# Three hand-written lists of steps set anew in the sparse and dense stage of a four-block network

## The chip, the cores and the metric

The kernel runs on one core of a Trainium2 chip. The metric is the device time of one execution in microseconds, and it is the median of a few executions that counts. The engines of the core run side by side and are tied together by semaphores alone: TensorE (PE, with its weight loads as PEld), VectorE (DVE), ScalarE (ACT), GpSimd (POOL), and SyncE (SP), which issues most of the transfers.

## The reference

The input is `x` of 8 x 512 tokens by 256 channels. Four residual blocks follow one another:

```python
x = x + attn(layernorm(x))                 # 16 heads, softmax; queries outside the 60% sparsest give 0
x = x + ffn(layernorm(x))                  # router picks 4 of 16 blocks of 64 hidden units; relu
x = x + gla(layernorm(x))                  # rms norm, gated linear attention over t = 8 steps,
                                           # then a gated FFN: silu(n @ w_gate.T) * (n @ w_up.T) @ w_down.T
x = x + ffn(layernorm(x))                  # the same sparse FFN once more

def step(S, qkva):                         # the recurrence of gla, t = 0..7, for 512 rows at once
    S = a_t[..., None] * S + k_t[..., :, None] * v_t[..., None, :]
    return S, einsum('bhk,bhkv->bhv', q_t, S)
```

The recurrence runs over the first axis of `x`, which has only 8 entries, so it is computed as sums over pairs of steps.

## The kernel before

The attention stage comes first and ends at about 546 us. It is not touched. Everything behind it is `block_part`. There the work is cut into named **steps**, such as `f1.d3`. A step has one part for each engine that has something to do in it. Every engine walks the same list of names and executes its own parts in the order of that list, one after the other (`run`, L1416 to L1438). An engine never changes places in its own order: if its next part waits for a semaphore, all that stands behind it on this engine waits too. So the lists are a schedule written out by hand, and only the relative places of steps that share an engine matter.

There are three lists. `START` (L1126 to L1157, 366 steps) opens the stage, `MERGED` (L1170 to L1176, 78 steps) is the body of a loop of five rounds, and `CLOSE` (L1177 to L1186, 109 steps) ends it.

**Steps of the attention's output, groups 0 to 7 of 512 tokens, in two sets of buffers s = 0, 1.** `p{s}.mask` (DVE, `masked`, L1579 and L1581) scales and masks the attention sums into `tok[s]`. `p{s}.T` transposes it on PE (L1919), and ACT and DVE split it into a high and a low half (L1821/1823, L1627). `p{s}.wo` is 24 matmuls (L1944). `p{s}.x` adds a bias on POOL (L1484) and the result on DVE (L1590).

**Steps of the sparse FFN.** `f{s}.ln` is a layer norm on DVE (L1595 to L1603), with a power on POOL (L1445) in the middle and the add of a bias on POOL (L1490) behind it. `f{s}.T` transposes. `f{s}.rt` is the router on PE (L1973), `f{s}.lg` the choice of four on DVE (L1645 to L1657), `f{s}.mk` the transposed mask. `f{s}.m0c`, `m1c` and `m0` to `m7` are the eight hidden blocks: six matmuls and one that adds the mask (L1933, L1991), relu on ACT (L1840), low half on DVE (L1773). `f{s}.d0` to `d7` are 12 matmuls each (L1961), and `d{m}` waits for the low half of `m{m}`. `f{s}.end` adds the sum to `x` on DVE (L1636).

**Steps of the gated linear attention.** `z.ln`, `z.rms`, `z.T` normalise and transpose a block. `z.o0` to `z.o8` are nine projections in one ring of two banks: `z.o3` is the gate (`gate_in`, L1690 and L1691, on DVE), `z.o7` and `z.o8` end in a sigmoid on ACT (L1851). `og` is an output gate (24 matmuls, L1944). `rec0` to `rec7` are the recurrence. In `rec{t}` DVE first makes the product for `t + 1` (L1700), which needs the decayed keys from POOL (L1509), PE sums over heads (L2030), and DVE multiplies and reduces (L1718, L1720). `o.mean`, `o.ln`, `o.T`, `o.wo`, `o.rms` (L1613 to L1616) are what follows. `o.x` adds `x` and `y` on POOL (L1525).

**Steps of the gated FFN.** `g.m{m}` and `g.u{m}` are six matmuls each; silu on ACT (L1862), product and rounded copy on DVE (L1780, L1786), low half on POOL (L1536). `g.d{m}` waits for this low half. The steps `e.*` are those of the last block, with `e.x` for `o.x` (L1530), `e.rms` for `o.rms` and `e.gT` for `g.T`.

**Weights.** `wt0` to `wt12` round the weights of the later blocks on ACT (L1830) and take the low half on POOL (L1471). `wt2` has 18 POOL instructions more in front of it, which centre the weight `wv`. `pads` clears four small tiles on POOL (L1478 to L1480), and SP waits for it before it loads the last eight pieces, which `wt10` to `wt12` read.

In a round of the loop the gated FFN and the last sparse FFN of one block (`g.*`, `f1.*`) run beside the linear attention of the next (`z.*`, `rec*`). `rec7` and the `o.*` steps of a block stand in the round after its `rec0` to `rec6`.

Of the kernel before, what the change touches and what calls it, by code (L numbers as in the profile page):

```python
# [1108 lines left out]
def merged(a, b, places):  # L1109

    out, n = [], 0
    for k, name in enumerate(a):
        while n < len(b) and places[n] <= k:
# [12 lines left out]
START = ["p0.mask", "p1.mask", "p0.T", "p1.T", "init0", "p0.wo", "p1.wo", "p0.x", "f0.ln", "f0.T", "f0.rt",  # L1126
# [40 lines left out]

BEFORE = list(counted(START))

# [33 lines left out]

FINAL = [closing(name) for name in CLOSE]

# [995 lines left out]
```

## Time and profile before

| | |
|---|---|
| median of three executions | 1591.77 us (1589.9 to 1596.35) |
| the profiled execution | 1595.34 us |
| its span | 1593.6 us |
| PE busy | 1484.4 us, 93% |
| DVE busy | 1103.1 us, 69% |
| ACT busy | 665.2 us, 42% |
| POOL busy | 550.3 us, 35% |
| mean granted TensorE clock | 0.971 of full speed |

The profiled execution lies 3.57 us above the median, within the spread of the three. Its span begins and ends with the first and last recorded work, and 1.74 us of its time lie outside. A line of the timeline reads: start in us, duration in us, engine, line, operation, written tile <- read tiles, how often; in brackets the idle time in front of it and what ended it. Where several instructions are merged, the duration covers all of them.

### The profile page before, as it was taken

The page shows a single profiled execution, that of the slowest core. Times are in us where ns is not written, and L with a number is a line of the kernel's source. Part 1 is how long each engine was busy: PE and PEld are TensorE (multiplying, and loading weights), DVE is VectorE, ACT ScalarE, POOL GpSimd, SP SyncE. Part 2 cuts the span into 40 slices and gives each one's busy share as a digit, 9 for nine tenths or more (in the row PEclk, how much of TensorE's full clock was granted, in tenths as well). Part 3 has the DMA queues.
Part 4 walks back from the last instruction along what each step waited for, and adds up shares of the span by engine and source line. Part 5 has one row for each costly group of instructions (what it writes and reads, how often), then busy time and mean ns, then how long its engine had stood idle before and what let it go on. Part 6 is the DMA issues. An engine that isn't in the chain of part 4 may idle for free.

```text
span 1593.6 us, 25605 instructions
## 1 busy us (share of the span) xinstructions
PE 1484.4 (93%) x8904; PEld 1060.6 (67%) x8904; DVE 1103.1 (69%) x2111; ACT 665.2 (42%) x970; POOL 550.3 (35%) x696
## 2 busy tenths in 40 slices
PE   8889999999997789999988899999999999999898
PEld 7434344434332368888867587878778787878787
DVE  6777887887878755555666777767676767767542
ACT  1567767767664522223234232424334243432211
POOL 6345544546531023214320433323222332322420
PEclk9899999999997889999999999999999999999999
DMA  4323223223221211100110100001010010100001
GB/s 130 88 58 76 60 57 74 63 59 70 47 57 35 91 45 40 54 27 28 35 41 14 27 1 23 19 1 39 0 39 0 13 26 0 39 0 14 14 1 27
DMA packets 56414, 61.04 MB, mean 38 GB/s; under 512 B 15733, under 2 KB 41637, under 8 KB 56349
## 3 DMA queue, kind: packets, MB, share of 16 engines
q1 hardware_dynamic: 42653, 43.89, 10.4%
q0 software_dynamic: 13408, 16.29, 4.8%
q8 instruction: 40, 0.66, 0.2%
q14 instruction: 25, 0.20, 0.0%
q10 hardware_dynamic: 288, 0.00, 0.0%
HBM read 25.51 MB, written 8.90 MB: 22 GB/s over the span
## 4 chain that ended last, share of the span: by engine, by line
PE 48%; issue 22%; DVE 13%; POOL 9%; ACT 5%; DMA 2%; SPq 1%; POOLq 0%; DVEq 0%; ACTq 0%
PE ps L1933 11%; PE ps L1961 8%; PE ps L922 6%; PE ps L935 6%; PE ps L908 3%; POOL h L1536 3%; PE ps L865 3%; DVE mc L613 3%; POOL kT L1509 2%; PE ps L1944 2%; PE ps L877 2%; PE ps L1973 2%; PE ps L1919 1%; ACT pT0b L797 1%; DVE oT_b L1720 1%
## 5 line engine op out<-in xcount | busy, mean ns | idle before, releaser
L613 DVE TENSOR_REDUCE mc<-ps 128x2 f32<-128x1024 f32 x256 | 302.8, 1219 | 52.1 <-PE ps L908 51.9
L1961 PE MATMUL ps<-w_hi,h 128*128 128x256 f32 x1024 | 218.2, 297 | 12.2 <-DVE h L1773 12.2
L1840 ACT ACTIVATE h<-ps 128x512 fp32r<-128x512 f32 x128 | 75.5, 598 | 320.5 <-PE ps L1991 320.4
L349 POOL DMA_DIRECT2D k_st<-k_hi x256 | 124.0, 490 | 188.5 <-PE ps L922 110.3
L1961 PEld LDWEIGHTS ps<-w_hi,h 128*128 128x128 f32 x1024 | 165.5, 188 | 18.8 <-DVE h L1773 17.9
L1773 DVE SCALAR_TENSOR_TENSOR h<-ps,h 128x512 fp32r<-128x512 f32 x128 | 87.1, 689 | 127.8 <-ACT h L1840 125.0
L1933 PE MATMUL ps<-xT_b,w_hi 128*128 128x512 f32 x512 | 171.1, 415 | 0.0
L1536 POOL TENSOR_TENSOR h<-hf,h 128x512 fp32r<-128x512 f32 x56 | 72.4, 1293 | 249.7 <-DVE h L1786 249.7
L922 PE MATMUL ps<-q_st,k_st 64*128 64x512 f32 x512 | 126.1, 490 | 23.3 <-ACT pT0b L797 7.8
L1961 PE MATMUL ps<-w_lo,h 128*128 128x256 f32 x512 | 142.9, 279 | 0.0
L922 PEld LDWEIGHTS ps<-q_st,k_st 64*128 64x128 f32 x512 | 49.3, 190 | 138.0 <-ACT pT1b L797 36.8
L1509 POOL TENSOR_TENSOR kT<-kT,aT 128x128 f32<-128x128 f32 (+6 forms) x56 | 72.0, 1285 | 172.1 <-DVE pr L1700 98.6
L908 PE MATMUL ps<-k_st,q_st 48*128 48x512 f32 x512 | 109.4, 447 | 22.8 <-DVE mc L613 9.8
L1933 PEld LDWEIGHTS ps<-xT_b,w_hi 128*128 128x128 f32 x512 | 91.2, 191 | 17.9 <-issue 2.7
L1933 PE MATMUL ps<-xT_b,w_lo 128*128 128x512 f32 x256 | 102.3, 400 | 0.0
L1961 PE MATMUL ps<-w_down_b_hi,h 128*128 128x256 f32 x512 | 102.1, 284 | 0.0
L1961 PEld LDWEIGHTS ps<-w_lo,h 128*128 128x128 f32 x512 | 96.2, 188 | 2.5
L908 PEld LDWEIGHTS ps<-k_st,q_st 48*128 48x128 f32 x512 | 48.6, 188 | 72.2 <-DVE mc L613 36.6
L1933 PE MATMUL ps<-xT_b,w_gate_b_hi 128*128 128x512 f32 x256 | 83.3, 407 | 3.7 <-DVE xT_b L1627 3.1
L1961 PEld LDWEIGHTS ps<-w_down_b_hi,h 128*128 128x128 f32 x512 | 82.5, 188 | 4.5 <-POOL h L1536 2.8
L797 ACT ACTIVATE pT0a<-ps 128x1024 f32<-128x1024 f32 x64 | 65.5, 1023 | 41.2 <-PE ps L922 39.5
L797 ACT ACTIVATE pT1b<-ps 128x1024 f32<-128x1024 f32 x64 | 65.5, 1023 | 39.5 <-PE ps L922 39.4
(270 smaller groups left out, 3422.2 us busy)
## 6 DMA issues: line engine op xcount, KB each, us to landing
q_st<-q_hi SPq DMA_DIRECT2D x256, 32.0 KB, 2.1
k_st<-k_hi POOLq DMA_DIRECT2D x256, 32.0 KB, 1.9
q_st<-q_lo SPq DMA_DIRECT2D x128, 32.0 KB, 2.0
k_st<-k_lo POOLq DMA_DIRECT2D x128, 32.0 KB, 1.9
x<-in_x_dram SPq DMA_DIRECT2D x8, 512.0 KB, 4.0
x_dram<-x SPq DMA_DIRECT2D x8, 512.0 KB, 2.9
yn<-x_dram SPq DMA_DIRECT2D x16, 256.0 KB, 3.9
x<-x_dram SPq DMA_DIRECT2D x16, 256.0 KB, 3.7
```

The lines of the kernel that those rows point to most:

```text
L349: eng.dma_start((q_st, k_st)[which][par][64 * e + DH * r:64 * e + DH * r + DH, j, :].bitcast(F32), src[(2 * j + e) * DH:(2 * j + e + 1) * ...
L613: v.tensor_reduce(mc[par][:, qt, 2 * HU + j:MC:NPAIR], ps[:, at:at + 2, :], AX_X, ALU.max).then_inc(max_done, 1)
L797: a.activation(pT[p % 2][half][:, :, :], ps[:, at:at + 2, :], ACT.Exp).then_inc(exp_done, 1)
L908: last = t_.matmul(bank[2 * odd + e][:, :], q_st[par][64 * e:64 * e + 3 * DH, j, qt * P:(qt + 1) * P], k_st[par][64 * e:64 * e + 3 * DH, j ...
L922: last = t_.matmul(bank[pair_at(u, half) + e][:, :], k_st[par][64 * e:64 * e + 64, j, kt * P:(kt + 1) * P], q_st[par][64 * e:64 * e + 64, ...
L935: last = t_.matmul(o_bank[at:at + OR, :], vz[g][:, kt, HG * gr + q, :], pT[p % 2][q // 2][:, q % 2, :], start=kt == 0, stop=kt == NT - 1, ...
L1509: g.tensor_tensor(keys, keys, decay, ALU.mult).then_inc(R["kd"], 1)
L1536: g.tensor_tensor(lo[:, :], hf[s][m % 2][:, :], hi[:, :].bitcast(F32), ALU.subtract).then_inc(S["hl"], 1)
L1773: v.scalar_tensor_tensor(lo[:, :], ps[:, RING[s] + m % 2, :], 0.0, hi[:, :].bitcast(F32), ALU.max, ALU.subtract).then_inc(F[s]["hl"], 1)
L1840: a.activation(h[s][m % 2][0][:, :], ps[:, RING[s] + m % 2, :], ACT.Relu).then_inc(F[s]["relu"], 1)
L1933: last = t_.matmul(ps[:, bank, :], ws[a][:, c, m * P:(m + 1) * P], xT[s][k][:, c, :], start=n == 0, stop=close and n == NC * len(PASSES) - 1)
L1961: last = t_.matmul(ps[:, ACC[s] + t // 2, (t % 2) * D:(t % 2 + 1) * D], h[s][m % 2][a][:, t * P:(t + 1) * P], ws[k][:, m, :], start=m == 0 ...
```

## The change

No step is added, removed or altered. The three lists are replaced by permutations of themselves. `MERGED` and `CLOSE` are given whole, from `START` the stretches that the text speaks of.

```diff
 START = [
...
-         "f0.m6", "f0.d5", "f1.m0c", "wt1", "f1.mk", "f0.m7", "f0.d6", "f1.m1c", "f1.m0", "f0.d7", "f0.end",
-         "p0.mask", "f1.m1", "f1.d0", "wt2", "f1.m2", "f1.d1", "f1.m3", "p0.T", "f1.d2", "f1.m4", "p0.wo",
...
-         "f1.d7", "f0.lg", "f0.m0c", "f1.end", "f0.mk", "f0.m1c", "p1.mask", "f0.m0", "p1.T", "wt3", "f0.m1",
...
+         "f0.m6", "f1.m0c", "f1.mk", "f0.d5", "f0.m7", "f1.m1c", "f0.d6", "f1.m0", "f0.d7", "f0.end", "f1.m1",
+         "f1.d0", "f1.m2", "f1.d1", "p0.mask", "f1.m3", "p0.T", "f1.d2", "f1.m4", "p0.wo", "p0.x", "f0.ln",
+         "f1.d3", "f1.m5", "f1.d4", "f1.m6", "f0.T", "f1.d5", "f1.m7", "wt1", "f0.rt", "f0.lg", "f0.m0c",
+         "f1.d6", "f1.d7", "f1.end", "f0.mk", "f0.m1c", "p1.mask", "f0.m0", "f0.m1", "p1.T", "f0.d0", "wt2",
...
-         "p1.mask", "f0.m1c", "z.ready", "wt8", "f0.m0", "p1.T", "f0.m1", "pads", "f0.d0", "p1.wo", "f0.m2",
-         "p1.x", "f0.d1", "f0.m3", "f0.d2", "f1.ln", "f0.m4", "f0.d3", "wt9", "f0.m5", "f1.T", "z.ln", "z.rms",
-         "f0.d4", "wt10", "f0.m6", "f0.d5", "wt11", "f1.rt", "f0.m7", "f1.lg", "f1.m0c", "f0.d6", "f0.d7",
-         "wt12", "z.T", "f0.end", "f1.m1c", "f1.mk", "z.o0", "z.o1", "z.o2", "og", "z.o3", "z.o4", "f1.m0",
-         "z.o5", "z.o6", "z.o7", "z.o8", "rec0", "f1.m1", "f1.d0", "rec1", "rec2", "rec3", "f1.m2", "rec4",
-         "f1.d1", "rec5", "f1.m3", "f1.d2", "z.y", "rec6", "rec7", "f1.m4", "f1.d3", "o.mean", "o.ln", "f1.m5",
-         "f1.d4", "f1.m6", "o.T", "f1.d5", "z.ln", "o.wo", "z.rms", "f1.m7", "f1.d6", "z.T", "f1.d7", "f1.end",
-         "z.o0", "og", "z.o1", "z.o2", "z.o3", "z.o4", "o.rms", "z.o5", "z.o6", "g.T", "z.o7", "z.o8", "g.m0",
-         "rec0", "g.u0", "g.m1", "rec1", "o.x", "g.u1", "g.d0", "rec2", "g.m2", "rec3", "rec4", "rec5", "rec6",
-         "g.u2", "g.d1", "rec7", "g.m3", "z.y", "g.u3", "o.mean", "g.d2", "o.ln", "g.m4", "g.u4", "g.d3",
...
+         "f0.m1c", "z.ready", "f0.m0", "f0.m1", "p1.T", "wt8", "f0.d0", "f0.m2", "f0.d1", "f0.m3", "p1.wo",
+         "p1.x", "f0.d2", "wt9", "f1.ln", "f0.m4", "f0.d3", "pads", "f0.m5", "f1.T", "z.ln", "z.rms", "f0.d4",
+         "f0.m6", "wt10", "f0.d5", "f0.m7", "f1.rt", "f1.lg", "f1.m0c", "f0.d6", "wt11", "f0.d7", "wt12", "z.T",
+         "f0.end", "f1.m1c", "f1.mk", "z.o0", "z.o1", "z.o2", "og", "z.o3", "z.o4", "f1.m0", "z.o5", "z.o6",
+         "z.o7", "z.o8", "rec0", "f1.m1", "rec1", "f1.d0", "rec2", "rec3", "rec4", "rec5", "f1.m2", "f1.d1",
+         "z.y", "rec6", "rec7", "f1.m3", "f1.d2", "o.mean", "o.ln", "f1.m4", "f1.d3", "f1.m5", "o.T", "z.ln",
+         "f1.d4", "o.wo", "z.rms", "f1.m6", "f1.d5", "f1.m7", "z.T", "f1.d6", "z.o0", "og", "z.o1", "z.o2",
+         "z.o3", "z.o4", "o.rms", "f1.d7", "f1.end", "g.T", "z.o5", "g.m0", "g.u0", "g.m1", "z.o6", "o.x",
+         "g.u1", "z.o7", "z.o8", "rec0", "rec1", "g.d0", "rec2", "rec3", "rec4", "g.m2", "rec5", "rec6", "g.u2",
+         "g.d1", "rec7", "g.m3", "z.y", "g.u3", "o.mean", "o.ln", "g.d2", "g.m4", "g.u4", "g.d3", "g.m5",
...
 MERGED = ["g.T", "rec7", "g.m0", "g.u0", "o.x", "g.m1", "g.u1", "g.d0", "g.m2", "g.u2", "o.mean", "g.d1", "z.y",
-          "o.ln", "g.m3", "g.u3", "g.d2", "g.m4", "o.T", "g.u4", "g.d3", "g.m5", "z.ln", "g.u5", "g.d4", "o.wo",
-          "g.m6", "z.rms", "g.u6", "g.d5", "z.T", "g.m7", "g.u7", "z.o0", "g.d6", "g.d7", "g.end", "z.o1",
-          "z.o2", "f1.ln", "z.o3", "z.o4", "z.o5", "f1.T", "z.o6", "z.o7", "f1.rt", "z.o8", "f1.lg", "og",
-          "f1.m0c", "f1.m1c", "f1.mk", "rec0", "rec1", "f1.m0", "f1.m1", "rec2", "f1.d0", "rec3", "f1.m2",
-          "f1.d1", "rec4", "f1.m3", "f1.d2", "f1.m4", "rec5", "f1.d3", "f1.m5", "f1.d4", "f1.m6", "f1.d5",
-          "rec6", "f1.m7", "f1.d6", "o.rms", "f1.d7", "f1.end"]
-CLOSE = ["g.T", "rec7", "g.m0", "g.u0", "g.m1", "g.u1", "o.mean", "g.d0", "o.ln", "g.m2", "g.u2", "g.d1",
-         "g.m3", "g.u3", "o.T", "g.d2", "g.m4", "g.u4", "g.d3", "g.m5", "g.u5", "g.d4", "g.m6", "g.u6", "g.d5",
-         "g.m7", "o.x", "g.u7", "z.y", "o.wo", "g.d6", "g.d7", "e.rms", "e.gT", "e.x", "g.end", "e.m0", "e.u0",
-         "e.m1", "e.u1", "e.d0", "f1.ln", "e.m2", "e.u2", "e.d1", "f1.T", "e.m3", "e.u3", "f1.rt", "f1.lg",
-         "e.d2", "f1.m0c", "e.m4", "e.u4", "f1.mk", "e.d3", "e.m5", "f1.m1c", "e.u5", "e.d4", "e.m6", "f1.m0",
-         "e.u6", "f1.m1", "e.d5", "e.m7", "f1.d0", "e.u7", "e.d6", "f1.m2", "e.d7", "e.gend", "e.ln", "f1.d1",
-         "f1.m3", "f1.d2", "f1.m4", "e.T", "f1.d3", "f1.m5", "e.rt", "f1.d4", "e.lg", "f0.m0c", "f1.m6",
-         "f0.mk", "f1.d5", "f0.m1c", "f0.m0", "f0.m1", "f1.m7", "f0.d0", "f0.m2", "f1.d6", "f0.d1", "f0.m3",
-         "f0.d2", "f0.m4", "f0.d3", "f0.m5", "f0.d4", "f0.m6", "f0.d5", "f0.m7", "f1.d7", "f0.d6", "f1.end",
-         "f0.d7", "e.end"]
+          "o.ln", "g.m3", "g.u3", "g.d2", "g.m4", "g.u4", "o.T", "g.d3", "g.m5", "z.ln", "g.u5", "o.wo", "g.d4",
+          "g.m6", "g.u6", "z.rms", "g.d5", "g.m7", "g.u7", "z.T", "g.d6", "g.d7", "z.o0", "g.end", "z.o1",
+          "f1.ln", "z.o2", "z.o3", "z.o4", "f1.T", "z.o5", "z.o6", "z.o7", "f1.rt", "z.o8", "f1.lg", "og",
+          "f1.m0c", "f1.m1c", "f1.mk", "rec0", "rec1", "f1.m0", "rec2", "f1.m1", "f1.d0", "rec3", "f1.m2",
+          "rec4", "f1.d1", "f1.m3", "f1.d2", "f1.m4", "rec5", "f1.d3", "f1.m5", "rec6", "f1.d4", "f1.m6",
+          "f1.d5", "f1.m7", "o.rms", "f1.d6", "f1.d7", "f1.end"]
+CLOSE = ["g.T", "rec7", "g.m0", "g.u0", "g.m1", "g.u1", "g.d0", "g.m2", "g.u2", "g.d1", "g.m3", "g.u3",
+         "o.mean", "o.ln", "g.d2", "g.m4", "g.u4", "g.d3", "g.m5", "g.u5", "g.d4", "g.m6", "g.u6", "o.T",
+         "g.d5", "z.y", "g.m7", "o.wo", "o.x", "e.rms", "g.u7", "e.gT", "g.d6", "g.d7", "e.x", "g.end", "e.m0",
+         "e.u0", "e.m1", "e.u1", "e.d0", "f1.ln", "e.m2", "e.u2", "e.d1", "f1.T", "e.m3", "e.u3", "f1.rt",
+         "e.d2", "f1.lg", "e.m4", "f1.m0c", "e.u4", "f1.mk", "f1.m1c", "e.d3", "e.m5", "f1.m0", "e.u5", "f1.m1",
+         "e.d4", "e.m6", "e.u6", "f1.d0", "e.d5", "e.m7", "e.u7", "e.d6", "f1.m2", "e.d7", "e.gend", "e.ln",
+         "f1.d1", "f1.m3", "f1.d2", "f1.m4", "e.T", "f1.d3", "f1.m5", "f1.d4", "e.rt", "e.lg", "f1.m6",
+         "f0.m0c", "f0.mk", "f1.d5", "f0.m1c", "f0.m0", "f0.m1", "f1.m7", "f0.d0", "f0.m2", "f0.d1", "f0.m3",
+         "f0.d2", "f0.m4", "f0.d3", "f0.m5", "f0.d4", "f0.m6", "f1.d6", "f0.d5", "f0.m7", "f1.d7", "f0.d6",
+         "f1.end", "f0.d7", "e.end"]
```

## Rows read from the trace of the kernel before

**Rows 1.** The page's first part: busy time, share of the span, number of instructions
```profile
PE 1484.4 (93%) x8904; PEld 1060.6 (67%) x8904; DVE 1103.1 (69%) x2111; ACT 665.2 (42%) x970; POOL 550.3 (35%) x696
```

**Rows 2.** Busy time by stage, with granted clock: opening chain, two rounds, closing list
```profile
core 0: us, PE busy (x) PEld busy (x) DVE busy (x) ACT busy (x) POOL busy (x), PEclk, DMA share, GB/s
810.80:928.10 117.30, 100.81 (x531) 78.91 (x530) 86.56 (x150) 37.56 (x66) 34.50 (x27) 0.94 0.07 19
981.91:1076.09 94.18, 91.71 (x530) 76.74 (x529) 66.13 (x135) 32.97 (x53) 28.37 (x21) 0.98 0.07 18
1076.09:1168.69 92.60, 90.21 (x530) 75.27 (x529) 65.99 (x135) 32.98 (x53) 28.36 (x21) 1.00 0.07 17
1448.06:1593.60 145.54, 134.16 (x806) 113.82 (x804) 67.33 (x155) 32.63 (x58) 33.27 (x23) 0.97 0.06 15
```

**Rows 3.** The chain that ended last, near 610 us: six and twelve matmuls undisturbed
```profile
610.21 1.40 PE ps L1933 x6
...
612.72 1.42 PE ps L1961 x12
```

**Rows 4.** Timeline of the round from 1076.09: the two stalls of TensorE (router, d7)
```profile
1130.51 1.95 PE L1973 MATMUL ps<-w_r,xT_b 128*128 128x32 f32 x16 [0.82 <-DVE xT_b L1627]
...
1167.17 0.39 PE L1961 MATMUL ps<-w_hi,h 128*128 128x256 f32 x1 [0.78 <-DVE h L1773]
```

**Rows 5.** The same round, VectorE: the gate and f1.T, then rec6 and m7
```profile
1126.38 2.76 DVE L1691 TENSOR_TENSOR gT<-w,gT 64x512 fp32r<-64x512 f32 x1
1129.17 1.29 DVE L1627 SCALAR_TENSOR_TENSOR xT_b<-ps,xT_b 128x512 fp32r<-128x512 f32 x2
...
1164.51 1.80 DVE L1720 TENSOR_REDUCE oT_b<-w 128x128 f32<-128x896 f32 x1
1166.42 0.69 DVE L1773 SCALAR_TENSOR_TENSOR h<-ps,h 128x512 fp32r<-128x512 f32 x1
```

**Rows 6.** The same round, GpSimd: low half of u7, then f1.ln's bias
```profile
1116.98 1.29 POOL L1536 TENSOR_TENSOR h<-hf,h 128x512 fp32r<-128x512 f32 x1 [3.80 <-DVE h L1786]
...
1126.08 2.50 POOL L1490 TENSOR_TENSOR x<-x,b_all 128x1024 f32<-128x1024 f32 x1 [1.50 <-DVE tok L1603]
```

**Rows 7.** Second recurrence of the opening list: GpSimd
```profile
880.64 2.38 POOL L1525 TENSOR_TENSOR x<-x,y 128x1024 f32<-128x1024 f32 x1
885.49 1.26 POOL L1536 TENSOR_TENSOR h<-hf,h 128x512 fp32r<-128x512 f32 x1 [2.47 <-DVE h L1786]
```

**Rows 8.** The same recurrence: VectorE, then TensorE at rec3
```profile
880.72 2.71 DVE L1700 TENSOR_TENSOR pr<-kT,qT 128x384 f32<-128x384 f32 x1 [2.10 <-POOL kT L1509]
...
887.74 0.69 DVE L1700 TENSOR_TENSOR tok<-kT,qT 128x512 f32<-128x512 f32 x1 [2.33 <-POOL kT L1509]
...
888.49 2.08 PE L2030 MATMUL ps<-tok,head_sum 128*128 128x256 f32 x4 [2.69 <-DVE tok L1700]
```

**Rows 9.** First recurrence of the opening list, VectorE between rec3 and rec4
```profile
823.20 0.69 DVE L1773 SCALAR_TENSOR_TENSOR h<-ps,h 128x512 fp32r<-128x512 f32 x1 [1.56 <-ACT h L1840]
```

**Rows 10.** Closing list: TensorE at e.gT, and VectorE's last part of e.rms
```profile
1492.70 1.97 PE L1919 MATMUL ps<-ident,tok 128*128 128x128 f32 x8 [3.37 <-DVE tok L1616]
...
1489.76 2.89 DVE L1616 TENSOR_SCALAR tok<-y,rinv 128x256 f32<-128x256 f32 x4
```

**Rows 11.** Sparse groups: p0.mask beside wt2, the wait behind it, a mask undisturbed
```profile
605.66 2.22 DVE L1581 TENSOR_TENSOR tok<-oa,share 128x1024 f32<-128x1024 f32 x1
...
608.53 0.39 PE L1961 MATMUL ps<-w_hi,h 128*128 128x256 f32 x1 [1.18 <-DVE h L1773]
...
634.84 1.22 DVE L1581 TENSOR_TENSOR tok<-oa,share 128x1024 f32<-128x1024 f32 x1
```

**Rows 12.** pads, the last of the eight loads behind it, low halves of m6 and m7
```profile
769.51 0.56 POOL L1478 MEMSET w_g<- 128x256 f32 x2 [3.65 <-PE ps L1944]
...
773.67 0.42 SPq L1360 DMA_DIRECT2D bg<-in_bg_dram  x1
...
790.20 1.28 DVE L1773 SCALAR_TENSOR_TENSOR h<-ps,h 128x512 fp32r<-128x512 f32 x2
```

More of the change, by code:

```diff
@@ L1123 @@
 W_STREAM.insert(W_STREAM.index("g.u1") + 1, "o.x")
-START = ["p0.mask", "p1.mask", "p0.T", "p1.T", "init0", "p0.wo", "p1.wo", "p0.x", "f0.ln", "f0.T", "f0.rt",
[31 rows of a table removed]
+START = ["p0.mask", "p1.mask", "p0.T", "p1.T", "p0.wo", "init0", "p1.wo", "p0.x", "f0.ln", "f0.T", "f0.rt",
[31 rows of a table added]
 def counted(names):
```

35 rows, old and new, of the table START are left out of this document.

## The prediction, made before the changed kernel was run

> **What bounds the kernel now.** I read the first part of the page, then the busy time by stage, then the chain that ended last, and then the timelines of those places where TensorE stands still. The reader is to see first that TensorE is busy for 93% of the span and no other engine for more than 69% [rows 1], and then that this is not spread evenly. In a round of the loop it is busy for 90.21 of 92.60 us, while in the opening list's stretch from 810.8 to 928.1 us, where two recurrences run with little other work beside them, it is busy for only 100.81 of 117.30 us [rows 2]. The closing list lacks 11.4 of 145.5 us [rows 2]. The chain names one step of TensorE after another where nothing stalls: 1.40 us for six matmuls and 1.42 us for twelve [rows 3]. A changed order leaves this work as it is, so all it can win or lose is the time in which TensorE waits, and the clock. The sum is therefore one of waits removed and waits made.
>
> **The loop, five rounds.** A round has two stalls that the timeline shows: 0.82 us ahead of the router and 0.78 us ahead of `f1.d7` [rows 4]. The modelled end of the matmul in front hides about 0.15 us more of each, as the idle time is counted from that end.
>
> *Router.* `f1.rt` waits for the low half of `f1.T`, which VectorE ends at 1130.46. It was held up by the gate's second instruction, 2.76 us [rows 5], which lies beside the bias add on GpSimd from 1126.08 to 1128.58 [rows 6]. The new list keeps five projections between `g.d7` and `f1.T`, so VectorE's row of work (`g.end`, `f1.ln`, gate, `f1.T`) starts and ends as before. Behind `f1.T` it has three projections in place of two (`z.o5` moved), so TensorE comes 1.40 us later [rows 3] to the same data. The stall of 0.82 us goes, with 0.4 us to spare: -0.8 to -1.0.
>
> *`f1.d7`.* It waits for the low half of `m7`, which stood behind `rec6` on VectorE: that ends at 1166.31, the low half runs from 1166.42 to 1167.11, the matmul starts at 1167.17 [rows 4, 5]. In the new list `rec6` comes ahead of `f1.d4`, and nothing stands ahead of `m7` but its own relu: -0.8 to -0.9. Late next are `m6` and `d6`, since `m6` is now behind `rec6`. From the end of `m5` to the start of `d6` TensorE has `rec6` and four steps, some 7.2 us at 1.4 to 1.6 us a step. In this time relu (0.6), the low half of `m5` (0.69), `rec6` (4.6) and the low half of `m6` (0.69) have to pass [rows 5], 6.6 us. It fits by about half a microsecond.
>
> *A wait made.* `g.d7` needs the low half of `u7` from GpSimd, which ended at 1118.27 [rows 6]. So far `z.o0` and `d6` (2.8 us) covered it almost exactly. Now it is `z.T`, eight transposes, and `d6`. The transposes took 1.97 us at half clock [rows 10], so 0.9 to 1.0 at full, where the projection took 1.40. `g.d7` waits: +0.5. `z.T` itself is safe: its `z.rms` comes one step later on VectorE, and it comes two steps later on TensorE. `z.o0` now has `d6` and `d7` behind `z.T`, as much as `m7` and `u7` gave.
>
> Per round -0.8 - 0.8 - 0.1 + 0.5 = -1.2, and five rounds make **-6.0**. Bounds: -2.0 a round if all of it goes and `d7` is covered after all, +0.5 if both stalls only move. `u4`/`o.T`, `d4`/`o.wo`, `m1`/`rec2` and `d1`/`rec4` change places between steps that have their data: nothing. Their cover is VectorE's idle share of 29% [rows 2].
>
> **The opening recurrences.** In the first, VectorE waited 1.56 us and spent 0.69 us on `f1.m2` between `rec3` and `rec4` [rows 9], since TensorE, at half clock, was late with it. The new list has `rec2` to `rec5` in one run: the chain ends 2.2 us earlier, while TensorE has done 3.1 us less of filling work (`f1.m3`, `f1.d2` go behind `rec7`). That work then stands in front of `o.T`, `o.wo` and `z.T`, where it covers waits; I take this as +0.9 at first and -1.3 by `z.o0`. In the second recurrence, GpSimd had to do the low half of `u0`, then `o.x` (2.38 us) and the low half of `u1` (1.26 us) between the decays of the keys [rows 7], and VectorE waited for these 2.10 and 2.33 us and took 2.71 us for a product beside `o.x`; TensorE stood still for 2.69 us at `rec3` alone [rows 8]. All three now come ahead of `rec0`, under the last projections. In exchange the sigmoids come behind four more steps, 4 x 1.40 = 5.6 us. Of 2.10 + 2.33 + 2.1 (the product stretched) = 6.5 us in the chain, 0.9 are left over. With the 2.2 us of the first recurrence `o.mean` comes 3.1 us earlier with the same work behind it. `z.o0` of the third block then waits 0.6 us, as only `g.d6` covers `z.T`, and `g.u7` ahead of `z.T` takes away some 0.5. Sum **-3.0**. Bounds: half of the stage's idle 16.5 us [rows 2] is the most that I would give, so -8. On the other side, the granted clock was 0.94 there [rows 2], that is two stretches of some 7 us at 1.2 GHz, each behind idle time of TensorE. One more such stretch over dense work costs half of it, +3.5.
>
> **Sparse groups.** `f1.d1` waited 1.18 us, because `p0.mask` (0.27 + 2.22 us) stood ahead of the low half of `m1` [rows 11]. It now stands two lows later, and `p0.T` waits some 0.8 us for it: -0.6. `wt2` moves beside the second group's `p1.mask`, which has 1.4 + 0.2 us less of TensorE's work in front of `p1.T` than before. The mask takes 1.22 us alone and 2.22 us beside `wt2` [rows 11]: +1.0 by the rows. The Trainium skill (GPSIMD Engine Reference, Specifications) has GpSimd's SBUF interfaces shared with VectorE, with contention for instructions with two SBUF inputs. The mask is such an instruction, so the page speaks against this move, and this trace agrees (2.22 against 1.22 us); a sum without contention would be 1.0 us lower. `wt9` no longer stands between `f1.ln` and `z.ln` on GpSimd, so the low halves of `m6` and `m7` no longer come as late as 790.20 [rows 12]: -1.4. `pads` moves from 769.51 to behind `f1.ln`'s bias, about 782. The eight loads take 3.7 us to issue (the last at 773.67 [rows 12]) and some 2 us to land, so `wt10` can start at 788.5, and the relu of `m7` is queued behind it on ScalarE. VectorE comes to `m7` at about 789 because of `z.rms`: nothing, and 1.6 us if that cover goes. The other moves of `wt` put 1.3 to 2.4 us of GpSimd ahead of a bias add that is waited for; 0.3 us each at two places. Sum **-1.0**, bounds -3 and +2.
>
> **Closing list.** TensorE stood still for 3.37 us ahead of `e.gT`; the last part of `e.rms` took 2.89 us, where `e.x` ran beside it on GpSimd [rows 10], and a further wait of 1.5 us followed ahead of `e.m0`. `e.x` now comes later: -1.75, down to the 1.14 us of such an instruction in a round. `g.d6` and `g.d7` go behind `e.gT` and cover the second wait: -1.5. Between `o.wo` and `e.gT` stands only `g.u7`: +1.4. At half clock, which follows such a wait, `d6` and `d7` cost 0.9 more. Sum **-1.0**, bounds -2.5 and +1.
>
> **Sum.** -6.0 - 3.0 - 1.0 - 1.0 = -11.0 us against the profiled 1595.34: 1584.3. The median of the runs shown is 3.57 us lower, so the predicted median is 1591.77 - 11.0 = 1580.8.
>
> **The rivals.** A measurement of this kernel can tell about 0.5%, 8.0 us, from no change.
>
> *Gains given back (chance 0.25).* The new order moves waits rather than removing them: `o.T` still waits for `o.ln`, `d6` takes the place of `d7`, and TensorE idles more in the recurrences, so that one more half-clock stretch comes. For it: the rounds already run at 97% of TensorE [rows 2], and half a microsecond of slack is thin. Against it: the two stalls of a round have one cause each, and both are undone. Half of the loop and none of the opening: -3 - 1 = -4, 1587.8.
>
> *More than forecast (0.09).* The round from 981.91 took 94.18 us at a granted clock of 0.98, the next 92.60 at 1.00 [rows 2]; one more of the five is like the first. If the half-clock stretches come from the stall at the router, both go: -3.1 more, and with the loop's -2.0 a round it is -18, 1573.8.
>
> *The loop turns slower (0.08).* Place: `rec5` and `rec6` now run back to back on VectorE. If they and the low halves between them take over half a microsecond longer than computed, `f1.d6` waits for `m6`. The recurrence has shown waits of up to 2.69 us for TensorE [rows 8]. One such wait in each round gives 5 x (0.5 + 2.69 - 0.9) = +11.5, and with the other parts at -5 the kernel ends at +6.5, 1598.3. Against it: VectorE has 29% of a round free.
>
> **Chances.** The forecast has 0.58, with a range of its own from -7 to -15. Over 0.5% faster: 0.54 of it, all of the second rival and a little of the first, 0.66. Over 0.5% slower: half of the last, 0.04. Within 0.5%: 0.30. The range from 1574 to 1591 leaves out the last rival, the upper end of the first and the far end of the second.
>
> **What the changed profile would show.** Right: rounds of 91.4 us in place of 92.6, no wait ahead of the router and `f1.d7`, and one of 0.5 us ahead of `g.d7` released by GpSimd; no `o.x` between the decays of the second recurrence; the stage behind 810.8 some 3 us shorter; `e.rms` ending in 1.14 us. Wrong: a wait of `f1.d6` for VectorE in each round, a granted clock under 0.92 in the opening recurrences, or ScalarE waiting for the transfer ahead of `wt10` with TensorE waiting for `m7`.

## The result, and the profile of the changed kernel

The changed kernel takes 1583.29 us in the median of nine executions (1577.63 to 1587.51), the kernel before 1596.35 us in nine beside it (1589.90 to 1599.77). The ratio is 0.9917, with a 95% interval of 0.9899 to 0.9936: some 13.2 us faster, between 10.2 and 16.1. The profiled execution has a span of 1581.5 us at a mean granted clock of 0.975, where the one before had 1593.6 us at 0.971, so 12.1 us are to be found in the rows.

First the page's busy times of the changed kernel. They answer to [rows 1]: each engine has the work that it had, within 3 us.

```profile
PE 1481.4 (94%) x8904; PEld 1058.9 (67%) x8904; DVE 1100.3 (70%) x2111; ACT 665.6 (42%) x970; POOL 549.7 (35%) x696
```

Then the busy time by stage with the granted clock behind it, of the changed kernel: two rounds of the loop, the closing list, and the opening list from 547.57 us on.

```profile
core 0: us, PE busy (x) PEld busy (x) DVE busy (x) ACT busy (x) POOL busy (x), PEclk, DMA share, GB/s
980.98:1072.33 91.35, 90.27 (x530) 75.13 (x529) 66.68 (x135) 33.06 (x53) 28.23 (x21) 1.00 0.07 18
1072.33:1163.71 91.38, 90.39 (x530) 75.22 (x529) 66.73 (x135) 33.09 (x53) 28.25 (x21) 1.00 0.07 17
1437.78:1581.50 143.72, 133.91 (x806) 113.29 (x804) 65.42 (x155) 32.45 (x58) 33.13 (x23) 0.98 0.06 15
547.57:980.98 433.41, 406.02 (x2477) 341.65 (x2478) 271.80 (x676) 126.00 (x212) 127.72 (x102) 0.96 0.12 37
```

And the same view of the kernel before, for the opening list and two rounds that [rows 2] does not show.

```profile
548.19:981.91 433.72, 406.98 (x2476) 339.98 (x2477) 276.30 (x676) 126.01 (x212) 126.61 (x102) 0.96 0.12 37
...
1168.69:1262.84 94.15, 91.76 (x530) 76.83 (x529) 66.09 (x135) 32.97 (x53) 28.37 (x21) 0.98 0.06 17
1262.84:1355.46 92.62, 90.22 (x531) 75.27 (x529) 66.00 (x135) 32.99 (x53) 28.35 (x21) 1.00 0.07 17
```

The five rounds took 466.15 us and take 456.80 (980.98 to 1437.78): 9.35 less. Of that, 5 x 1.24 = 6.2 come from 92.60 against 91.36 us, and 3.1 from two rounds of 94.2 us, at a granted clock of 0.98, that have no successor. The closing list gives 1.82, the opening list only 0.31 and the untouched attention stage 0.62. These are the 12.1.

Inside a round the changed kernel shows no idle time at the router, and a short one at `g.d7`. The first of the following lines is TensorE's router, the second the first matmul of `g.d7`, the third GpSimd's low half of `u7`, which released it; the last two are VectorE's last part of `rec6` and the low half of `m6` behind it.

```profile
1126.30 1.95 PE L1973 MATMUL ps<-w_r,xT_b 128*128 128x32 f32 x16
```
```profile
1113.73 0.39 PE L1961 MATMUL ps<-w_down_b_hi,h 128*128 128x256 f32 x1 [0.27 <-POOL h L1536]
```
```profile
1112.38 1.29 POOL L1536 TENSOR_TENSOR h<-hf,h 128x512 fp32r<-128x512 f32 x1 [2.91 <-DVE h L1786]
```
```profile
1156.70 1.79 DVE L1720 TENSOR_REDUCE oT_b<-w 128x128 f32<-128x896 f32 x1
1158.61 0.69 DVE L1773 SCALAR_TENSOR_TENSOR h<-ps,h 128x512 fp32r<-128x512 f32 x1
```

One more wait stands in the round, at `f1.d0`, for the low half of `m0`. The kernel before had it as well, as a third stall beside the two of [rows 4]. The first line is of the kernel before, the second of the changed one.

```profile
1141.69 0.39 PE L1961 MATMUL ps<-w_hi,h 128*128 128x256 f32 x1 [0.69 <-DVE h L1773]
```
```profile
1137.49 0.38 PE L1961 MATMUL ps<-w_hi,h 128*128 128x256 f32 x1 [0.49 <-DVE h L1773]
```

The low half of `m6` ends at 1159.30 and `f1.d6` starts at 1160.42, so the slack that I had put at half a microsecond is 1.1 us. `f1.d7` follows with nothing in front of it.

In the first opening recurrence something new stands. Here is VectorE in `rec2` of the changed kernel, then TensorE just before, with `f1.d0` (first and last line of nine) between `rec1` and `rec2`.

```profile
816.17 0.69 DVE L1700 TENSOR_TENSOR tok<-kT,qT 128x512 f32<-128x512 f32 x1 [0.37 <-POOL kT L1509]
818.75 0.56 DVE L1718 TENSOR_TENSOR w<-ps,vT 128x384 f32<-128x384 f32 x1 [1.89 <-PE ps L2030]
```
```profile
813.65 1.22 PE L2030 MATMUL ps<-tok,head_sum 128*128 128x128 f32 x4 [2.42 <-DVE tok L1700]
814.52 0.56 PE L1961 MATMUL ps<-w_hi,h 128*128 128x256 f32 x1
...
817.01 0.41 PE L1961 MATMUL ps<-w_hi,h 128*128 128x256 f32 x1
817.23 1.48 PE L2030 MATMUL ps<-pr,head_sum 128*128 128x192 f32 x4
```

TensorE stands idle for 2.42 us, then does `f1.d0`, and only then the sums that VectorE waits for. In the old list `f1.d0` stood ahead of `rec1`, inside that idle time, of which 1.02 us were left.

The place of `f1.d0` is only half of the cause. From 812.44 to 819.27 the granted clock was 0.50 in this execution, and `f1.d0` took 2.9 us (814.52 to 817.43). Four of the kernels run later have the same opening list. In one the stretch at half clock was as long, and VectorE waited 1.89 us again. In two it was 3.4 us long and the wait 1.16 and 1.17 us. In the fourth, the changed kernel with `o.wo` drawn forward in its closing list, TensorE ran at full clock here, `f1.d0` took 1.66 us, and nothing waited. Here is the same instruction of VectorE in the kernel with the new opening list alone, and in that fourth one:

```profile
816.37 0.56 DVE L1718 TENSOR_TENSOR w<-ps,vT 128x384 f32<-128x384 f32 x1 [1.16 <-PE ps L2030]
```
```profile
817.75 0.55 DVE L1718 TENSOR_TENSOR w<-ps,vT 128x384 f32<-128x384 f32 x1
```

It is the same in the second recurrence, with `g.d0`: VectorE waits 1.03 to 1.15 us in the four with a stretch there, 1.06 of them in this one, and not at all in the one without.

The closing list still has its large wait. These are VectorE from `o.wo`'s add to `e.rms`, ScalarE's copy `z.y`, and TensorE at `e.gT`, to be read against [rows 10].

```profile
1475.44 1.29 DVE L1761 TENSOR_TENSOR y<-ps,y 128x512 f32<-128x512 f32 x2 [3.66 <-ACT y L1875]
...
1479.42 1.14 DVE L1616 TENSOR_SCALAR tok<-y,rinv 128x256 f32<-128x256 f32 x4
```
```profile
1474.35 1.06 ACT L1875 ACTIVATE y<-yn 128x1024 f32<-128x1024 f32 x1 [3.52 <-POOL x L1525]
```
```profile
1480.62 1.22 PE L1919 MATMUL ps<-ident,tok 128*128 128x128 f32 x8 [3.48 <-DVE tok L1616]
```

The last part of `e.rms` takes 1.14 us in place of 2.89, and nothing waits any more ahead of `e.m0`. But TensorE still stands still for 3.48 us, since only `g.u7` is left to do between `o.wo` and `e.gT`.

### The profile page after: what moved, and what is told of

Read it like the earlier page. It is cut to its first block, busy times and chain, and to the rows that moved or that the text cites. A ratio compares the mean times of both kernels' runs of the same rounds, so it can differ in the third digit from the quotient of the medians.

```text
span 1581.5 us, 25604 instructions
## 1 busy us (share of the span) xinstructions
PE 1481.4 (94%) x8904; PEld 1058.9 (67%) x8904; DVE 1100.3 (70%) x2111; ACT 665.6 (42%) x970; POOL 549.7 (35%) x696
## 3 DMA queue, kind: packets, MB, share of 16 engines
q1 hardware_dynamic: 42653, 43.89, 10.5%
## 4 chain that ended last, share of the span: by engine, by line
PE 54%; issue 19%; DVE 11%; POOL 8%; ACT 5%; DMA 1%; SPq 1%; POOLq 0%; DVEq 0%; ACTq 0%
PE ps L1933 15%; PE ps L1961 10%; PE ps L935 5%; PE ps L922 5%; PE ps L908 3%; POOL h L1536 3%; DVE mc L613 3%; PE ps L865 3%; PE ps L1944 2%; PE ps L877 2%; POOL kT L1509 2%; PE ps L1919 2%; ACT pT0b L797 1%; PE ps L1973 1%; DVE oT_b L1720 1%
## 5 line engine op out<-in xcount | busy, mean ns | idle before, releaser
L613 DVE TENSOR_REDUCE mc<-ps 128x2 f32<-128x1024 f32 x256 | 303.0, 1219 | 51.1 <-PE ps L908 50.7
L349 POOL DMA_DIRECT2D k_st<-k_hi x256 | 123.5, 488 | 188.0 <-PE ps L922 109.8
L1961 PE MATMUL ps<-w_down_b_hi,h 128*128 128x256 f32 x512 | 106.1, 291 | 1.6 <-POOL h L1536 1.5
L1862 ACT ACTIVATE hf<-ps 128x512 f32<-128x512 f32 x56 | 33.5, 598 | 121.4 <-PE ps L1933 121.4
```

What stands on the lines that cost most here:

```text
L349: eng.dma_start((q_st, k_st)[which][par][64 * e + DH * r:64 * e + DH * r + DH, j, :].bitcast(F32), src[(2 * j + e) * DH:(2 * j + e + 1) * ...
L613: v.tensor_reduce(mc[par][:, qt, 2 * HU + j:MC:NPAIR], ps[:, at:at + 2, :], AX_X, ALU.max).then_inc(max_done, 1)
L1961: last = t_.matmul(ps[:, ACC[s] + t // 2, (t % 2) * D:(t % 2 + 1) * D], h[s][m % 2][a][:, t * P:(t + 1) * P], ws[k][:, m, :], start=m == 0 ...
```

## The experiments

The first three runs put one new list at a time into the kernel before; nothing else differs.

> The kernel before with the new list of the loop round alone. Theory A (the gain is the loop's own: two waits less in each of five rounds, and the half-clock stretches that followed the router's wait in two of them): 9.3 us less than before, rounds of 91.4 us, no stretch at 1.2 GHz between 982 and 1440 us. Rival B (where a half-clock stretch falls hangs on what the opening list has done to the phase of the work, so it was the new opening list that took the two away): 6.2 us less, with rounds of 91.4 us but for one or two of 93.

> The kernel before with the new opening list alone. Theory A: within 1 us of before, as the changed trace shows 0.3 us less between 548 and 982 us; the rounds keep their 92.6 us, and two of them their 94.2. Rival B: 3 us less, the rounds all at 92.6 us. My prediction had 4 us less for this part.

> The kernel before with the new closing list alone. Theory A: 1.8 us less, with a wait of 3.6 us left ahead of the e.gT step and none ahead of e.m0, and 3.4 us at half clock behind it in place of 6.8. If the closing list gained only because it came after other rounds, nothing.

| kernel | ratio to before | 95% interval | profiled: opening from `z.T`, five rounds |
|---|---|---|---|
| new loop list alone | 0.9934 | 0.9921 to 0.9947 | 186.50, 456.55 us |
| new opening list alone | 0.9980 | 0.9966 to 0.9993 | 186.8, 467.94 us |
| new closing list alone | 0.9968 | 0.9954 to 0.9982 | 188.0, 466.23 us |

The loop list alone gives 10.5 us of 1597.74, with five rounds of 91.27 to 91.34 us. The two long rounds are gone although the opening list is the old one, and with the new opening list alone two rounds stay long (95.8 and 94.2 us). So rival B of these texts falls: the gain of the loop is the loop list's own. The opening list alone is worth 3.2 us (1.1 to 5.4), the closing list 5.1 (2.9 to 7.3). In single profiles these two show 1.4 and 2.9 us of span. Stretches of a few us at half clock fall differently from one execution to the next, and the untouched attention stage alone ended between 544.8 and 549.7 us in the thirteen profiles. The interval of the closing list lies above the 1.8 us that its stage shows, and why is open. The three parts make 18.8 us, the whole change 13.2 (10.2 to 16.1). With an uncertainty of over 2 us in each part that is no proof that they hinder each other, nor that they add up.

To find which wait brought the half clock into the rounds, the loop list was cut in two at `rec0`, and each half run with the other half old.

```
e4_front: new up to f1.mk   (... g.m7 g.u7 z.T g.d6 g.d7 z.o0 ... z.o4 f1.T z.o5 z.o6 z.o7 f1.rt ...), old behind
e11_rear: old up to f1.mk, new from rec0 on (... f1.m5 rec6 f1.d4 f1.m6 f1.d5 f1.m7 o.rms f1.d6 f1.d7)
```

> The kernel before with the new loop list up to the first recurrence step and the old one from there. Theory A: the router's wait goes (0.9 us a round), the wait of g.d7 for GpSimd comes (0.45), and both half-clock stretches of the loop go, since each stood behind the router's wait: 5 x 0.45 + 3.1 = 5.4 us less, rounds of 92.2 us. Rival (the stretches stood behind the sum of a round's waits, the one of f1.d7 among them): only 2.2 us less, one or two rounds of 93.7 us.

> The kernel before with the old loop list up to the first recurrence step and the new one from there, the complement of the run with the front half alone. Theory A (half-clock stretches of the loop stand behind the router's wait, which stays): the wait of f1.d7 goes, the router's 0.8 us stays, rounds of 91.8 us but for one or two of 93.3: 5 x 0.85 = 4.2 us less and no more. Rival (a stretch needs the sum of a round's waits, whichever go): no stretch left in the loop, 7.3 us less.

The front half alone: ratio 0.9951 (0.9934 to 0.9968). The rear half alone: 0.9983 (0.9967 to 0.9998). The busy time by stage, of two rounds of the kernel with the new front half,

```profile
981.42:1073.61 92.19, 90.20 (x527) 75.17 (x529) 66.85 (x135) 32.97 (x53) 28.24 (x21) 1.00 0.07 18
1073.61:1165.75 92.14, 90.22 (x528) 75.19 (x529) 66.88 (x135) 32.98 (x53) 28.23 (x21) 1.00 0.07 17
```

and of three rounds of the one with the new rear half, with 6.8 us cut out of the last of them:

```profile
980.63:1074.15 93.52, 91.69 (x528) 76.82 (x529) 65.95 (x135) 33.05 (x53) 28.33 (x21) 0.98 0.07 18
1074.15:1165.96 91.81, 90.05 (x527) 75.27 (x529) 65.83 (x135) 33.05 (x53) 28.35 (x21) 1.00 0.07 17
...
1257.75:1352.58 94.83, 93.08 (x527) 78.25 (x529) 65.96 (x135) 33.06 (x53) 28.35 (x21) 0.96 0.07 17
```
```profile
1313.50:1320.30 6.80, 6.80 (x32) 6.70 (x32) 3.21 (x21) 2.02 (x3) 0.00 (x0) 0.50 0.00 0
```

The last line has a granted clock of 0.50, that is 1.2 GHz, while TensorE is busy from end to end. Just before it stands this one, the router of that round:

```profile
1312.17 2.43 PE L1973 MATMUL ps<-w_r,xT_b 128*128 128x32 f32 x16 [0.82 <-DVE xT_b L1627]
```

A round without a stretch at half clock is 0.47 us shorter by the front half (92.60 to 92.13) and 0.80 by the rear half (to 91.80). The front half removes the stretches, though `f1.d7` still waits; the rear half removes that wait and keeps them, three in five rounds here. Over all profiles, the kernels with the router's wait (the one before, the new opening and the new closing list alone, and the rear half) had 9 stretches in 20 rounds, each of them begun 1.0 to 2.9 us after the start of the router; the nine others had none in 45 rounds. So it is the front half that takes the stretches away. That it does so by the router's wait and not by another of its moves rests on where the nine began; the wait was not removed by itself.

The kernel with the rear half gained 2.7 us, with an interval of 0.3 to 5.3 that holds the 4.2 expected too. In its profile the five rounds took 465.24 us, 0.91 less than before, since it had three stretches for two.

Next, the step that I took to be at fault in the opening list was undone in the changed kernel, on its own:

```
- rec0 f1.m1 rec1 f1.d0 rec2            + rec0 f1.m1 f1.d0 rec1 rec2
- z.o8 rec0 rec1 g.d0 rec2              + z.o8 g.d0 rec0 rec1 rec2
```

> The changed kernel, with f1.d0 back ahead of rec1 in the first opening recurrence and g.d0 ahead of rec0 in the second. Theory A (the opening list gained next to nothing because these two steps, put between rec1 and rec2, hold up rec2 on TensorE and so VectorE, by 1.89 and 1.06 us): both waits of VectorE go, TensorE's wait of 2.6 us ahead of the first rec1 shrinks to 1.3, o.mean comes 1.5 us earlier in the first recurrence and, with it, 2.5 us earlier in the second; span 1579.0 against 1581.5. Rival (the chain is set by VectorE's own work and GpSimd's decays, and TensorE is late only where it does not matter): within 0.5 us of the changed kernel in that stage.

Ratio 0.9896 (0.9867 to 0.9924). Times of the whole do not tell it from the changed kernel; the profile does. VectorE in both `rec2` of this kernel:

```profile
817.30 0.55 DVE L1718 TENSOR_TENSOR w<-ps,vT 128x384 f32<-128x384 f32 x1
```
```profile
886.01 0.55 DVE L1718 TENSOR_TENSOR w<-ps,vT 128x384 f32<-128x384 f32 x1
```

Both waits are gone, though a stretch at half clock lies over both places (816.21 to 826.45, 884.47 to 887.89). Busy time by stage from the first `z.T` to the loop, of the kernel before, the changed one, and this one:

```profile
793.88:981.91 188.03, 170.23 (x932) 136.27 (x931) 131.87 (x243) 63.53 (x104) 49.28 (x38) 0.96 0.06 18
```
```profile
793.42:980.98 187.56, 168.45 (x933) 136.94 (x932) 130.03 (x244) 63.50 (x104) 49.32 (x38) 0.97 0.06 18
```
```profile
793.97:979.91 185.94, 169.82 (x925) 136.00 (x931) 129.79 (x243) 63.49 (x104) 49.30 (x38) 0.96 0.06 18
```

The stage is 1.6 us shorter here, not 2.5, and even that is not more than chance can give: the five profiles of the unchanged opening list took 185.8 to 187.7 us for it, and the shortest of them is the one whose `rec2` never waited. From the second `rec0` to `o.mean` this kernel took 23.97 us against 25.01, but that same profile took 24.18 with `g.d0` where it was. From the first `z.T` to `o.mean` it took 42.85 against 43.62 us, and the unchanged list took 42.7 to 42.9 in three of its five profiles. Behind `rec2` VectorE waits 0.70 us for GpSimd's decay of the keys (819.17), and this execution had 10.2 us at half clock there where the changed kernel had 6.8. So the run shows that the waits go when the two steps are moved. It doesn't show a gain in time, and at full clock there was no wait to remove. Its span was no shorter (1581.4 us): the closing list, with 6.8 us at half clock for 3.4, took 1.06 us more, and all that lies ahead of `z.T` 0.55 more.

Two runs asked whether the waits that the change left or made could go as well: in the loop those of `g.d7` and `f1.d0`, in the closing list the one at `e.gT`.

```
loop   - g.d5 g.m7 g.u7 z.T                                    + g.m7 g.u7 g.d5 z.T
       - f1.m0c f1.m1c f1.mk rec0 rec1 f1.m0 rec2 f1.m1 f1.d0  + f1.mk f1.m0c rec0 rec1 f1.m0 f1.m1c rec2 f1.m1 f1.d0
close  g.T rec7 g.m0 g.u0 g.m1 g.u1 o.mean g.d0 o.ln g.m2 g.u2 o.x g.d1 g.m3 g.u3 o.T g.d2 g.m4 g.u4
       g.d3 z.y g.m5 g.u5 o.wo g.d4 g.m6 g.u6 e.rms g.d5 g.m7 g.u7 e.gT (rest as it was)
```

> The changed kernel with two further edits of the loop list: g.d5 behind g.u7, so that the low half of u7 is earlier by a copy of 0.7 us, and f1.mk, rec0 and rec1 moved ahead of f1.m1c, so that the low half of m0 is there when f1.d0 comes. If the waits of a round are what the trace names (g.d7 for GpSimd 0.43, f1.d0 for VectorE 0.83), a round takes 90.1 to 90.3 us in place of 91.37, and the kernel 5.5 to 6.5 us less. If they only move: rounds of 91.4.

> The changed kernel with o.mean, o.T and o.wo drawn forward in the closing list, so that six steps of TensorE stand between o.wo and e.gT in place of one. The wait of 3.6 us ahead of e.gT goes and with it the half-clock stretch behind it: 3.6 + 0.9 = 4.5 us less, the closing list at 139.2 us. Rival (VectorE, which then has o.ln between two of the u steps, holds up the gates instead): 2 to 3 us less with new waits ahead of g.d1 or g.u3.

The loop: ratio 0.9837 (0.9810 to 0.9864), five rounds of 450.5 us in place of 456.8. A round of it, and the closing list of the other kernel (ratio 0.9866, 0.9834 to 0.9898), in the view of busy time by stage:

```profile
1068.84:1158.92 90.08, 89.98 (x528) 75.49 (x529) 66.71 (x135) 32.94 (x53) 28.26 (x21) 1.00 0.07 17
```
```profile
1436.81:1576.10 139.29, 131.88 (x799) 112.00 (x804) 66.80 (x155) 32.57 (x58) 33.17 (x23) 0.99 0.06 16
```

In the profiles both came out at the number forecast, 6.3 and 4.4 us less in the stage. (The medians, 1572.79 and 1577.90 us, can't check this as closely: the changed kernel was not run beside these two, and the kernel before spread from 1590.74 to 1604.25 there.) TensorE is now busy for 89.98 of 90.08 us in a round. In the closing list a wait of 1.13 us is left ahead of `e.gT`, which I had expected to go altogether, and the half-clock stretch behind it is gone.

Then the opening list set anew, which failed:

```
- ... f0.d0 wt2 f0.m2 ... p1.x f0.d3 f1.ln f0.m5    + ... f0.d0 f0.m2 ... p1.x f0.d3 f1.ln wt2 f0.m5
- z.rms f0.d4 f0.m6 f0.d5 f0.m7 ... f1.m0c ... z.T  + f0.d4 f0.m6 f0.d5 f0.m7 z.rms ... z.T f1.m0c
- rec0 f1.m1 rec1 f1.d0 rec2 ... f1.m2 f1.d1        + rec0 f1.m1c f1.m1 rec1 ... f1.d0 rec4 f1.m2 rec5 f1.d1
third block: from its z.T on as a round of the changed loop list, with both edits of the first of the two runs above
fourth sparse group: as in the kernel before but for wt7 (p0.wo, f0.T, f0.rt earlier, p1.mask later)
```

> The changed kernel with an opening list rearranged further: z.rms behind the low halves of m6 and m7, f1.m0c and f1.m1c out of the way of the first projections, the second expert steps spread over the gaps of the two recurrences, and the third block set like a round. Theory A (the chain of projections, recurrence and output is what counts, and TensorE's filling work must go where the chain waits for VectorE or GpSimd): o.mean 2.5 us earlier in the first recurrence and 4 us in the second, the stage from 548 to 982 us 4 to 6 us shorter. Rival (VectorE is saturated in the recurrences, so order does nothing): under 1.5 us.

Ratio 0.9951 (0.9930 to 0.9973), slower than the changed kernel. The profile puts it down to one step, `wt2`: up to the first `z.T` the stage took 253.89 us against 245.85. TensorE at `f0.d5`, ScalarE at `wt2`, and GpSimd beside them:

```profile
664.91 0.58 PE L1961 MATMUL ps<-w_hi,h 128*128 128x256 f32 x1 [9.52 <-DVE h L1773]
```
```profile
663.02 0.63 ACT L1830 ACTIVATE wv_b_hi<-wv_b_raw 128x512 fp32r<-128x512 f32 x1 [16.78 <-POOL wv_b_raw L1464]
663.55 1.07 ACT L1840 ACTIVATE h<-ps 128x512 fp32r<-128x512 f32 x2
```
```profile
653.87 2.36 POOL L1490 TENSOR_TENSOR x<-x,b_all 128x1024 f32<-128x1024 f32 x1 [1.50 <-DVE tok L1603]
...
656.51 4.73 POOL L1459 TENSOR_TENSOR v_mean<-v_mean,wv_b_raw 128x32 f32<-128x32 f32 x14
661.33 0.31 POOL L1461 TENSOR_SCALAR v_mean<-v_mean 128x32 f32<-128x32 f32 x1
```

GpSimd can start to centre `wv` only when `f1.ln`'s bias is done. ScalarE waits for it in its own order, and the relu of `m5` behind it. In the changed list GpSimd does this while it waits for work anyway. The kernel put together below has `wt2` where the changed list has it, and no such wait. Past that, the stage from `z.T` to the loop took 186.94 us, 0.6 less than in the changed kernel: the third block took 51.1 in place of 53.5 us, the two recurrences 1.7 us more, with `o.T` waiting 2.86 us (852.45) where it had waited 1.23 (844.04). Theory A's gain of 4 to 6 us did not come.

Last, what had gained was put together: both edits above, `f1.d0` and `g.d0` moved as shown, and the third block and the fourth sparse group as in the last run. The fourth group is thereby ordered as in the kernel before again, but for `wt7`: one part of the change is taken back. The changed kernel ran again beside it.

> The changed kernel with what the runs so far have shown to gain, together: the two further edits of the loop list (rounds of 90.1 us: 6.3 us less), o.wo drawn forward in the closing list (4.4 us less), f1.d0 and g.d0 out of the way of rec2 (1.7 us), and two parts of the rearranged opening list: the third block set like a round (2.4 us) and the fourth sparse group's router one step later (0.9 us). If they add up: a span of 1581.5 - 15.7 = 1565.8 us and a ratio to before of 0.982. If half-clock stretches come back elsewhere in exchange: 1568 to 1572.

> The changed kernel once more, on the chip and in the rounds of its successor: 0.9917 of before as measured at first, within 0.003, rounds of 91.4 us with no half-clock stretch in them. A half-clock stretch in a round would speak against the router's wait as what brings them about.

The sum: 1567.54 us, ratio 0.9823 (0.9795 to 0.9852), span 1562.7 us. The changed kernel: 1581.90 us, ratio 0.9903 (0.9875 to 0.9930), no stretch at half clock in its rounds. In the new kernel by stage, the opening from `z.T`, a round and the closing list:

```profile
789.61:972.70 183.09, 167.00 (x926) 134.38 (x931) 129.38 (x243) 63.38 (x104) 49.20 (x38) 0.98 0.07 18
```
```profile
972.70:1062.86 90.16, 90.00 (x528) 75.52 (x529) 66.67 (x135) 30.38 (x51) 28.21 (x21) 1.00 0.07 18
1423.22:1562.70 139.48, 131.73 (x799) 112.02 (x804) 66.63 (x155) 32.56 (x58) 33.15 (x23) 1.00 0.06 16
```

The span is 3.1 us below the 1565.8 expected if the parts add up. In the medians this kernel takes 14.4 us less than the changed one (15.7 had been expected), about as much again as the change had gained.

## Why the prediction was right, and where not

The forecast was 11.0 us less, and 13.2 (10.2 to 16.1) were measured. The absolute number, 1583.29 against 1580.8, is off by more in appearance, because the kernel before was itself at 1596.35 in this comparison and not at 1591.77. But that the sum came out near is in part luck: the loop gave 3.4 us more than forecast, and the opening recurrences and the sparse groups together 3.7 us less.

**Loop, forecast -6.0, shown -9.35.** The terms held. A round fell by 1.24 us where I had -1.2, to 91.4; the front half gave -0.47 (router gone, `g.d7` waits 0.27 us in the timeline, and some 0.15 more under the modelled end of the matmul in front) and the rear half -0.80. The stall did not move to `f1.d6`. But I read two stalls where the round had three: the 0.69 us at `f1.d0` were in the trace of before. They stayed, as 0.49 us at `f1.d0` and 0.13 ahead of the sums of `rec2`, and are part of what the run with the two further edits of the loop gained. The other 3.1 us are the mechanism of the second rival: the stretches at half clock stood behind the router's wait and went with the front half of the list. I had it right as a mechanism and gave it a chance of 0.09. The row that could have raised it was in the trace of before: both long rounds had their stretch within 3 us of the router's start (1036.40 and 1038.3, 1223.11 and 1226.0), and none had one behind `f1.d7`, which waited as long. My price for that rival, 18 us, held besides a loop of -2.0 a round, which nothing here supports.

**Opening recurrences, forecast -3.0, shown -0.5.** (The old opening list took 188.0 us from `z.T` to the loop in four profiles and 186.50 in a fifth, the new one 186.9 in the mean of five: 0.8 less.) This is the step that failed. For the first recurrence I took the chain to be 2.2 us shorter, since VectorE waited 1.56 us and spent 0.69 us on `f1.m2` between `rec3` and `rec4`. It is 0.9 (43.62 against 44.48 us from `z.T` to `o.mean`), for two reasons. The first is that the 1.56 us belonged to the clock and not to the list. The old opening list had 6.8 us at half clock there in four profiles, and this wait in each of them. In the fifth, the run with the new loop list alone, it ran at full clock, the same instruction of VectorE waited for nothing (817.01, below), and the old chain took 42.93 us. The new one took 42.73 in the profile whose only stretch came late (3.4 us at 823.11, at `rec4`). Like for like the new order is thus worth 0.9 us at half clock and 0.2 at full.

```profile
817.01 0.69 DVE L1773 SCALAR_TENSOR_TENSOR h<-ps,h 128x512 fp32r<-128x512 f32 x1
```

The second reason is that I followed what was moved out of VectorE's order and not what now stood in TensorE's: `f1.d0` went out of an idle time of 2.4 us into the one place where, at half clock, its 2.9 us delay `rec2`, by 1.89 us here. For the second recurrence, 7.0 us left the chain (32.04 to 25.01 us from `rec0` to `o.mean`), where I had 6.5; but the projections ahead of `rec0` took 6.8 us longer (from `z.T` 19.95 to 26.78) and not 5.6. The four steps are 5.6; most of the rest is a wait of 1.05 us ahead of `rec0` that I left out. The balance was to be -0.9 and is -0.2, and from that `o.mean` to the third block's `z.T` 0.7 us were given back. The sign that I had named, the stage behind 810.8 some 3 us shorter, did not show: from the first `rec0` to the third block's `z.T` it is 117.2 us against 117.3.

**Sparse groups, forecast -1.0, shown +0.2** (245.69 and 245.85 us from the first step to `z.T`). The terms that I listed make -0.4 and not -1.0, as the two of 0.3 us were left out of the sum. `f1.d1`'s wait went. The transposes behind the second group's mask wait, 0.70 us, so the size of my +1.0 was about right, but not for the cause that I gave. Here is VectorE's mask in the changed kernel and what GpSimd does beside it:

```profile
634.05 1.22 DVE L1581 TENSOR_TENSOR tok<-oa,share 128x1024 f32<-128x1024 f32 x1
```
```profile
634.24 1.19 POOL L1461 TENSOR_SCALAR v_mean<-v_mean 128x32 f32<-128x32 f32 x1
```

The mask took its undisturbed 1.22 us [rows 11]. GpSimd paid: 1.19 us for an instruction that took 0.31 without a mask beside it (661.33 in the run above). In the kernel before, the mask ran beside a large subtraction of GpSimd and was the one to be stretched. The Trainium skill (GPSIMD Engine Reference, Specifications), which I had weighed, says that the two share their SBUF interfaces. These rows agree, and show besides that either engine can be the one held up. Before, the mask began 0.15 us after GpSimd's instruction; here it began 0.19 us ahead of it. So it may be the later of the two that pays, but two pairs don't settle that. The 1.4 us at `f0.d6` did not come: TensorE had waited only 0.45 us there in the kernel before, so the term was too large from the start, and the wait is still there (0.43 us), since the low half of `m6` stands behind `z.rms` on VectorE whatever GpSimd does. And I missed the fourth group, where `f0.rt` and `f0.m0c` moved closer to what they wait for: the router there now waits 0.32 us (754.68), and 3.4 us at half clock at 757.8 followed, as in three of the five profiles of this list.

**Closing list, forecast -1.0, shown -1.8.** `e.rms` fell to 1.14 us and `d6` and `d7` covered `e.m0`'s wait, as computed. The gain came out larger because 3.4 us at half clock follow the wait where it had been 6.8, and I had added 0.9 for more of them. The length of that stretch varies with either list: over all profiles the old closing list took 145.5 to 147.0 us (five, with 6.8 or 10.2 us at half clock behind the wait) and the new one 143.7 to 144.9 (six, with 3.4 or 6.8). The wait at `e.gT` itself was to be 3.37 - 1.75 + 1.4 = 3.0 us and is 3.48: `o.wo`'s add waited 3.66 us for `z.y`, which waited for `o.x` on GpSimd, a queue that I had not followed here. The run with `o.wo` drawn forward shows what the wait was worth, 4.4 us.

**The other rivals.** The first named the right size for the opening list, where little was gained, and was wrong for the loop. Its reason, waits moved rather than removed, fits the second recurrence; of the first one's 2.2 us most had not been there to gain. The third has nothing for it: `f1.d6` starts without a wait in each round.

## What to carry to other kernels

Before a wait is priced, look whether it lies in a stretch at half clock. If it does, part of it may belong to the clock, and a second profile of the same kernel can be without it. Here that would have cut a term of 2.2 us to 0.2 to 0.9.

When steps of a fixed order are moved, write down for each engine what now stands in front of each waited-for instruction, not only what has left. A filler belongs into an idle time that is as long as itself and ahead of an instruction that is late anyway; one place further on it can delay the chain. A short wait of TensorE can cost more than its length: look for a drop of the granted clock behind it, and count that in the price of the wait before asking which of several equal waits to remove first.

## What the runs showed of the hardware

A wait of 0.82 us at the router was followed by 3.4 or 6.8 us at 1.2 GHz in 9 of 20 rounds; a wait of 0.78 us at `f1.d7` and one of 0.70 at `f1.d0`, in 15 of these rounds and five others, were followed by none. What tells them apart was not tried. The matmuls behind the waits follow each other alike, sixteen of the router in 1.95 us and twelve of a `d` step in 1.42 [rows 3, 4]; but the router's are of 32 elements and the others of 256.

The new opening list, run unchanged in five kernels, had 3.4 or 6.8 us at half clock in its first recurrence and none or 3.4 in the second, and took between 185.8 and 187.7 us from `z.T` to the loop. The attention stage, the same instructions in all thirteen profiles, ended between 544.8 and 549.7 us. A difference of under 2 us in such a stage is thus not to be read from one profile, and a wait of 1 to 2 us that borders on half clock can be gone in the next.
